# LSTM and state-space kernel: the recurrent matmuls of the second half repacked to 32 rows and 128 columns

## The reference

```python
# LSTM, T = 512 steps, h and c of [8, 512], Wh of [512, 2048]
xW = jnp.einsum('ntd,dg->ntg', x, Wx) + b
def step(carry, xw_t):
    prev_h, prev_c = carry
    a = xw_t + prev_h @ Wh
    i, f, o = sigmoid of a[:, :512], a[:, 512:1024], a[:, 1024:1536]
    g = jnp.tanh(a[:, 1536:])
    next_c = f * prev_c + i * g
    next_h = o * jnp.tanh(next_c)
x = x + lstm(x, cond, Wx, Wh, b)
# state-space layer on the new x
proj = conv(x) @ Wp + bp          # conv over time, taps from cond
B_t, C_t = softplus(proj[..., :64]), tanh(proj[..., 64:])
state = decay * state + dt * B_t * (x @ Ws + bs)
x = x + (C_t * state) @ Wo + bo
```

## Time and profile before

| | |
|---|---|
| median of 3 runs | 1964.98 us (1964.32 to 1966.52) |
| profiled execution | 1966.61 us, its span 1964.8 us |
| PE busy | 1791.0 us (91%) |
| DVE busy | 1431.2 us (73%) |
| ACT busy | 1047.5 us (53%) |
| mean granted TensorE clock | 0.994 |
| recurrent steps | first transpose of recA at 49.7 us, last at 1943.3 us |

### The profile page before, as it was taken

One profiled execution on the slowest core, in us unless ns is written; L12 is line 12 of the kernel. 1 busy time (PEld: TensorE's weight loads), 2 busy tenths in 40 slices (PEclk: granted clock), 3 DMA queues, 4 the chain that ended last, 5 costly groups with the idle time before them and its releaser, 6 DMA issues.

```text
span 1964.8 us, 90420 instructions
## 1 busy us (share of the span) xinstructions
PE 1791.0 (91%) x36274; PEld 1276.6 (65%) x36274; DVE 1431.2 (73%) x6909; ACT 1047.5 (53%) x4057; POOL 340.3 (17%) x1544
## 2 busy tenths in 40 slices
PE   6788999999999999999999999999999999999976
PEld 3555666676666666666676666666666677666755
DVE  7686667777777776777777777777777777867775
ACT  5555455555555555555555545555555555545452
POOL 1111111111111111111111111111111111111110
PEclk9999999999999999999999999999999999999998
DMA  6111111111211211111111111111111111211100
GB/s 233 49 43 47 36 46 35 51 50 36 56 51 35 62 43 49 46 46 52 45 54 39 57 44 42 55 43 48 46 53 46 44 54 32 70 43 40 51 14 23
DMA packets 112284, 98.71 MB, mean 50 GB/s; under 512 B 20097, under 2 KB 86197, under 8 KB 110838
## 3 DMA queue, kind: packets, MB, share of 16 engines
q1 hardware_dynamic: 111576, 90.83, 15.3%
q10 hardware_dynamic: 288, 2.10, 0.3%
HBM read 50.90 MB, written 41.94 MB: 47 GB/s over the span
## 4 chain that ended last, share of the span: by engine, by line
PE 45%; DVE 33%; ACT 11%; issue 5%; POOL 5%; DMA 1%; SPq 0%; POOLq 0%; DVEq 0%; ACTq 0%
PE recA L495 26%; DVE tr L848 17%; PE recB L495 9%; DVE pre L854 8%; ACT act L737 6%; POOL h L432 5%; PE pbc L540 4%; DVE hb L876 4%; PE pw L465 4%; ACT tc L747 3%; DVE prod L859 3%; ACT recB L664 1%; PE po L560 1%; DMA wpk<-in_L_cond_Wh_dram 1%; DVE acc L931 0%
## 5 line engine op out<-in xcount | busy, mean ns | idle before, releaser
L737 ACT ACTIVATE act<-pre 128x64 f32<-128x64 f32 x1024 | 263.0, 257 | 873.4 <-DVE pre L854 856.9
L495 PE MATMUL recA<-whi,hb 128*16 128x256 f16 x8176 | 514.8, 274 | 143.1 <-DVE hb L876 137.6
L495 PE MATMUL recA<-wlo,hb 128*16 128x256 f16 x8176 | 513.1, 273 | 0.0
L495 PE MATMUL recB<-wlo,hb 128*16 128x256 f16 x8176 | 513.0, 273 | 0.0
L495 PE MATMUL recB<-whi,hb 128*16 128x256 f16 x8176 | 513.0, 273 | 0.0
L495 PEld LDWEIGHTS recA<-whi,hb 128*16 128x16 f16 x8176 | 200.2, 88 | 410.3 <-DVE hb L876 354.4
L848 DVE STREAM_TRANSPOSE tr<-recA 128x256 f32<-128x256 f32 x512 | 229.9, 449 | 206.2 <-PE recA L495 205.0
L540 PE MATMUL pbc<-yt,wpk 128*128 128x256 f32 (+5 forms) x1120 | 333.3, 402 | 0.0
L432 POOL TENSOR_TENSOR h<-osc,tc 128x16 f32<-128x16 f32 x1024 | 228.2, 223 | 499.8 <-ACT tc L747 499.8
L426 POOL TENSOR_SCALAR osc<-act 128x16 f32<-128x16 f32 x512 | 105.1, 205 | 1098.4 <-ACT act L737 1098.4
L859 DVE SCALAR_TENSOR_TENSOR prod<-act 128x32 f32<-128x32 f32 x1024 | 197.1, 193 | 127.5 <-ACT act L737 127.5
(11 more groups left out here) (156 smaller groups left out, 2027.6 us busy)
## 6 DMA issues: line engine op xcount, KB each, us to landing
xw_rows<-xs SPq DMA_DIRECT2D x128, 256.0 KB, 2.2
seed<-xw_rows SPq DMA_DIRECT2D x1024, 32.0 KB, 1.9
xn<-in_x_dram SPq DMA_DIRECT2D x32, 256.0 KB
out_dram<-ot SPq DMA_DIRECT2D x32, 256.0 KB, 3.0
seed<-in_L_cond_Wh_dram ACTq DMA_DIRECT2D x2, 1024.0 KB, 6.9
wpk<-in_L_cond_Wh_dram SPq DMA_DIRECT2D x2, 1024.0 KB, 11.8
wlo<-in_L_cond_Wx_dram SPq DMA_DIRECT2D x2, 1024.0 KB, 13.1
xs<-in_L_cond_Wx_dram SPq DMA_DIRECT2D x1, 1024.0 KB, 9.3
```

The costliest lines, as they stand in the source:

```text
L495: ins = pe.matmul(rec[half][32 * j:32 * j + 2 * NB, 0:256].rearrange("p (c f) -> p c f", c=2), h[:, k, :], w[:, k, :, :].rearrange("p (c j ...
L737: act_eng.activation(act[q][:, 0:G, :].rearrange("p g n -> p (g n)"), pre[q][:, :, :, :].rearrange("p g c b -> p (g c b)"), ACT.Tanh, scal ...
```

## The change

Only half 1 is packed differently. Its two chunks no longer stand side by side as 256 columns in 16 of the 32 rows of a quadrant; chunk 2 takes rows 0 to 15 and chunk 3 rows 16 to 31 of each quadrant, and both take the same 128 columns. The matmul of one chunk has a stationary operand of 32 columns, of which 16 are zeros: `hz` has the 16 columns of the hidden state in the middle of 48, and a slice that starts at 16 (chunk 2) or 0 (chunk 3) puts them in the first or the last 16 rows. So each input chunk `k` of half 1 has four groups instead of two, of 128 moving columns instead of 256. A step has 96 matmuls instead of 64. `seeds` and `open_` of half 1 handle 128 columns, with a mask of its own. Of half 1's block with k 0, only chunk 2's part stays ahead of half 0's k 2 and 3; chunk 3's part stands behind them.

The diff, without the setup of the masks, the memsets and some renamings:

```diff
+        hz = [sb(f"hz{i}", [128, KC, 6 * NB], f16) for i in range(2)]
+        h0z = [sb(f"h0z{i}", [128, KC, 6 * NB], bf16) for i in range(2)]
...
+        tr = [sb("tr0", [128, 2, G, 4, NB]), sb("tr1", [128, G, 2, 2, NB])]
...
+        hb, h0b = ([h[:, :, 2 * NB:4 * NB] for h in hs] for hs in (hz, h0z))
+
+        WIDTH = (256, 128)
...
+        def first_seeds(eng, p, count):
+            for j in range(4):
+                own = slice(128 * j, 128 * j + 128)
+                rows = slice(2 * NB * p, 2 * NB * p + 2 * NB)
+                if count > 1:
+                    eng.dma_start(seed[32 * j:32 * j + 2 * NB, 0, p, :, :].rearrange("r q (c f) -> r (q c) f", f=128)[:, 0:count, :],
+                                  scratch[0, 0:count, rows, own].rearrange("c r f -> r c f")).then_inc(s_seed0[p], 16)
+                else:
+                    eng.dma_start(seed[32 * j + 2 * NB:32 * j + 4 * NB, 0, p, 1, 0:128],
+                                  scratch[0, KC - 1, rows, own]).then_inc(s_seed0[p], 16)
...
+                row, col = ((0, 128 * (c % 2)), (2 * NB * (c % 2), 0))[c // 2]
                 for j in range(4):
-                    sync.dma_start(seed[32 * j:32 * j + 2 * NB, z, :, c // 2, 128 * (c % 2):128 * (c % 2) + 128],
+                    sync.dma_start(seed[32 * j + row:32 * j + row + 2 * NB, z, :, c // 2, col:col + 128],
...
-            def recur(t, half, k):
+            def recur(t, half, k, parts=(0, 1)):
...
-                if k == 0:
+                if k == 0 and parts[0] == 0:
                     pe.wait_ge(s_seed[half], t + 1)
...
+                for h in (h0z if t == 0 else [hz[(t - 1) % 2]]):
+                    if half:
+                        for c in parts:
+                            for w in (whi, wlo):
+                                for j in range(4):
+                                    ins = pe.matmul(rec[1][32 * j:32 * j + 32, 0:128],
+                                                    h[:, k, 2 * NB * (1 - c):2 * NB * (1 - c) + 32], w[:, k, 4 * (2 + c) + j, :],
+                                                    start=False, stop=(k == KC - 1), skip_group_check=True)
...
                     recur(t, 0, 1)
-                    recur(t, 1, 0)
+                    recur(t, 1, 0, (0,))
                     recur(t, 0, 2)
                     recur(t, 0, 3)
+                    recur(t, 1, 0, (1,))
                     recur(t, 1, 1)
...
+                act_eng.activation(rec[q][:, 0:WIDTH[q]], seed[:, t // TS % 2, t % TS // 2, q, 0:WIDTH[q]],
+                                   ACT.Copy, scale=mask[:, q, t % 2:t % 2 + 1]).then_inc(s_seed[q], 1)
...
             wx_high(1)
+
+            act_eng.wait_ge(s_wlo, 1)
+            for c in range(KC):
+                act_eng.wait_ge(s_rows[c], 16)
+            first_seeds(act_eng, 0, 1)
...
+                order = ("p c g z b -> p (c g z b)", "p g c z b -> p (g c z b)")[q]
+                dve.transpose(tr[q][:, :, :, :, :].rearrange(order), rec[q][:, 0:WIDTH[q]]).then_inc(s_tr[q], 1)
...
+                if q:
+                    dve.tensor_tensor(pre[1][:, :, :, :], tr[1][:, :, :, 0, :],
+                                      tr[1][:, :, :, 1, :], ALU.add).then_inc(s_add[1], 1)
```

More of the change, by code:

```diff
@@ L387, in _ @@
             for p in range(TS // 2):
[L388 to L391, removed]
+                first_seeds(sync, p, KC - 1)
+                if p:
+                    first_seeds(sync, p, 1)
             for c in range(KC):
@@ L483, in first_project @@
                             x_bias(tile_bank(0, c)[:, :], c)
-            def recur(t, half, k):
+            def recur(t, half, k, parts=(0, 1)):
                 if half == 0 and k % 2 == 0:
                     pe.wait_ge(s_h[k // 2], t + 1)
-                if k == 0:
+                if k == 0 and parts[0] == 0:
                     pe.wait_ge(s_seed[half], t + 1)
[L492 to L498, removed]
+                for h in (h0z if t == 0 else [hz[(t - 1) % 2]]):
[6 more added lines that the diff above has]
+                                                    start=False, stop=(k == KC - 1), skip_group_check=True)
+                    else:
+                        for w in (whi, wlo):
+                            for j in range(4):
+                                ins = pe.matmul(rec[0][32 * j:32 * j + 2 * NB, 0:256].rearrange("p (c f) -> p c f", c=2),
+                                                h[:, k, 2 * NB:4 * NB],
+                                                w[:, k, :, :].rearrange("p (c j) f -> p c j f", j=4)[:, 0:2, j, :],
+                                                start=False, stop=(k == KC - 1), skip_group_check=True)
                 if k == KC - 1:
@@ L662, in seeds @@
                 if t < TS and t % 2 == 0 and q == 0:
[L663 to L665 removed]
+                    act_eng.wait_ge(s_seed0[t // 2], 16 * 8)
+                act_eng.activation(rec[q][:, 0:WIDTH[q]], seed[:, t // TS % 2, t % TS // 2, q, 0:WIDTH[q]],
+                                   ACT.Copy, scale=mask[:, q, t % 2:t % 2 + 1]).then_inc(s_seed[q], 1)
             def soft(key, name, src, bias, cols):
@@ L847, in open_ @@
                 dve.wait_ge(s_rec[q], t + 1)
-                dve.transpose(tr[q][:, :, :, :, :].rearrange("p c g z b -> p (c g z b)"),
-                              rec[q][:, 0:256]).then_inc(s_tr[q], 1)
+                order = ("p c g z b -> p (c g z b)", "p g c z b -> p (g c z b)")[q]
+                dve.transpose(tr[q][:, :, :, :, :].rearrange(order), rec[q][:, 0:WIDTH[q]]).then_inc(s_tr[q], 1)
             def add(t, q):
                 dve.wait_ge(s_tr[q], t + 1)
-                dve.tensor_tensor(pre[q][:, :, :, :].rearrange("p g c b -> p c g b"), tr[q][:, :, :, 0, :],
-                                  tr[q][:, :, :, 1, :], ALU.add).then_inc(s_add[q], 1)
+                if q:
+                    dve.tensor_tensor(pre[1][:, :, :, :], tr[1][:, :, :, 0, :],
+                                      tr[1][:, :, :, 1, :], ALU.add).then_inc(s_add[1], 1)
+                else:
+                    dve.tensor_tensor(pre[0][:, :, :, :].rearrange("p g c b -> p c g b"), tr[0][:, :, :, 0, :],
+                                      tr[0][:, :, :, 1, :], ALU.add).then_inc(s_add[0], 1)
             def product(t, q):
@@ L1015, in _ @@
             for z in range(2):
-                dve.tensor_reduce(mask[:, z:z + 1], diag[:, z:16:4], mybir.AxisListType.X, ALU.max).then_inc(s_mask, 1)
+                for q in range(2):
+                    dve.tensor_reduce(mask[:, q, z:z + 1], diag[:, z:16:4 - 2 * q], mybir.AxisListType.X,
+                                      ALU.max).then_inc(s_mask, 1)
             def largest(k):
@@ L1069, in _ @@
             dve.wait_ge(s_scale, 1)
-            for z in range(2):
-                dve.tensor_scalar(mask[:, z:z + 1], mask[:, z:z + 1], scale[:, 2:3], None, ALU.mult).then_inc(s_mask, 1)
+            for q in range(2):
+                dve.tensor_scalar(mask[:, q, :], mask[:, q, :], scale[:, 2:3], None, ALU.mult).then_inc(s_mask, 1)
             wh_high(2)
```

15 lines of the change are left out of this document (6 added, 9 removed).

## The result

The changed kernel takes 1935.39 us (median of 4 runs, 1934.36 to 1938.33), the one before 1964.65 (4 runs, 1964.32 to 1966.52): ratio 0.9852 [0.9835, 0.9869]. It is faster by 29 us; 37 were forecast (1928 us), and the time lies inside the forecast's own range of 1914 to 1948. The execution profiled took 1938.33 us, its span 1936.3.

The account below looks back on a forecast made before the run. In 341 steps PE waits, and the chain between recA transposes sets the time; elsewhere PE is full. 341 x 0.09 = 31 us plus 6 us gives 37: 1966.6 to 1929.6 profiled, 1928 as median; range 1914 to 1948, chance 0.77.

Parts of the forecast that it names:

- term 1: PE's filler before recA's third chunk: narrow groups 0.056 us apart, so it ends at +2.88 instead of +2.99.
- rival A: PE's narrow groups take 0.09 us each, not half the time; +0.40 a step, 2169 us; chance 0.13.
- term 2: Half 1's state: shorter ACT seeds let `tc` start at +2.12 and free the low part at +2.88, 0.09 earlier.
- terms 3 and 4: recB's transpose starts 0.13 us later, at +0.78, but takes 0.32 instead of 0.449, so product 0 stays at +1.03.
- The joint: Where product 0 on DVE follows recB's later transpose: slack of only 0.01 us, further delay there reaching both halves.
- D: Rival: group interval 0.058, transpose 0.34; 0.04 to 0.05 us lost a step, 17 us, 1948; within the range given 0.77.
- B: Rival: half 1's state comes no earlier; gain 0.02 us a step where PE waits, 1961 us; chance 0.07.
- C: Rival: full steps gain too and the joint costs nothing; 511 x 0.10 = 51 us, 1914; within the range given 0.77.
- The full steps: About 170 steps where PE's work decides: between a loss of 0.02 and a gain of 0.09 us, counted as 6 us.
- The rest: Small items: SP's 28 start transfers cause no wait; ACT's issues cost 0.3 us once, step 0's shorter groups returning about that.

Follow-up runs that it names:

- wide_seeds: The changed kernel with ACT's seeds of half 1 again 256 columns wide; 1960.49 us, ratio 0.9973 to the kernel before.
- wide_transpose: The changed kernel with DVE's transpose of half 1 again 256 columns wide; 1988.24 us, ratio 1.0114 to the kernel before.
- no_filler: The changed kernel with all of half 1's first block behind half 0; 1977.91 us, ratio 1.0062 to the kernel before.
- split_only: The kernel before, nothing packed, one of the two wide groups of half 1's first block moved behind half 0; 2010.95 us, ratio 1.0229.
- after_again: The changed kernel run again, unaltered, in a later sitting; 1934.53 us, ratio 0.984 to the kernel before.
- replan: The changed kernel with PE's beside work planned anew, same instructions in other steps; 1932.24 us, ratio 0.9832 to the kernel before.
- replan2: The changed kernel with replan's plan, but higher planner costs for `u` and `out`; 1929.65 us, ratio 0.9812 to the kernel before.

## Why the prediction came out as it did

- **The interval of narrow groups (term 1): right.** 0.056 us, over 14 groups in each of 511 steps (in step 0 part of them ran at a granted clock of 0.50). With it rival A is refuted. These groups follow neither of the two rules of the Trainium skill that spoke for it ("TensorE: Matmul & The Clock Gate", sections "Back-to-back issue gap" and "Wait — 56ns, not 53.3ns?"): four matmuls with four loads fit into 0.056 here, where the one rule gives 0.081 for a single pair and the other 0.100 for four matmuls. The four matmuls of a group, which write different quadrants, start within 0.010 us of each other in this trace, less than half of the second rule's floor for a single start.
- **The state of the second half (term 2): right in its mechanism, 0.02 too early at the end.** Seeds 354 ns (0.35), `tc` at +2.12. But `tc` lasts 216 ns where it lasted 199, and the low part starts at +2.67 instead of +2.65. These 17 ns are most of the difference between the 0.10 forecast and the 0.09 measured at +2.90. wide_seeds shows the term alone: 0.07 of 0.08.
- **The later end of recB and its shorter transpose (terms 3 and 4): right.** +0.78, 317 ns (0.32), product 0 at +1.03, second add at +1.14. The joint held, D did not come; wide_transpose, no_filler and split_only show what it costs when it gives way: 0.12, 0.10 and 0.09 a step.
- **B and C: neither.** The gain in steps with room is 0.08 to 0.085, against 0.02 (B) and 0.10 (C). The price of D was added up wrongly: 1928 + 17 is 1945, not 1948. The 3 us make the forecast's range wider than its terms; the measured time lies inside either way.
- **The full steps: this term was mis-sized.** "The middle gives 170 x 0.035 = 6 us"; the full steps measured 0. Two errors lie in it. First the bounds: a step that is full by a whole beside matmul can't gain, since its PE work grew by the 0.024 that the prediction itself worked out, and it lost 0.02; taking the middle between that and 0.09 had no row behind it. Second the count: the 341 of the earlier trace rows are the waits of more than 0.15 us, and the view does not give the length of each. PE had shorter ones in 69 more steps; what a step can gain is the smaller of 0.09 and its room. Sorted by room, 390 steps paid 31 us, and 121 paid nothing. That this equals the prediction's 341 x 0.09 = 31 us is luck: more steps gained, each somewhat less.
- **The rest:** 2.2 us at the end are put down to the clock, by the comparison above. SP's 28 transfers cost nothing that can be seen: they were issued by 56.9 us and the block for step 8 by 67.7 (forecast 65.0), and no step waits for them. Step 0 did not give back what the start cost, as the prediction had it; it took 0.4 us more, which is inside the 31.1.

So 37 became 28.5 in the profiled spans (29.3 between the medians of the runs): 6 us of full steps, 2.2 at the end, 0.4 at the start.

## What to carry to other kernels

Where two engines' work meets at one point, shorten both or neither. Here the packing alone gave nothing and the move alone cost 45 us; with both but the seeds left wide 5 us of gain remained, and with the transpose left wide the kernel was 22 us slower than before. All together gave 29 us. When a chain of steps gets shorter, list for every step how much room the busiest engine has, and count the gain step by step up to that room; beside work that was laid out for the old length of a step has to be laid out anew. When a move makes one piece later and a saving elsewhere makes it good, look for the instruction where the two meet, since from there on each ns costs about a ns in every step that has room. And before you count waits in a view, ask how short a wait it still lists.

## What the runs showed of the hardware

- The loads of 32 columns are busy for 97 ns each against 88 to 90 for 16 columns, and a group of four is issued every 56 ns: this work runs side by side and its busy time is no interval. By form, kernel after:

```profile
L515 PEld LDWEIGHTS recB<-whi,hz 128*32 128x32 f16 x16352 | 438.2, 97 | 10.1 <-issue 0.7
```

- Once, PE issued nothing for 0.86 us without a wait, inside the recurrent work, and the step took 4.48 us. Kernel after, timeline:

```profile
767.84 0.27 PE L521 MATMUL recA<-wlo,hz 128*16 128x256 f16 x1
...
768.70 0.28 PE L521 MATMUL recA<-wlo,hz 128*16 128x256 f16 x3 [0.58 <-issue]
```

Such waits inside the recurrent work, of 0.2 to 0.7 us, are listed once in this trace, three times in replan's, twice in replan2's and once in wide_seeds'. There are none in the other five traces of kernels with 96 matmuls a step (after_again's among them), and none in the three with 64. The queue of instructions moves more than before (414 packets, 6.78 MB, against 286 and 4.69), for 96 matmuls a step instead of 64. Whether the stall is a late supply of instructions was not tested and stays open. The listed waits come to 1.5 us at most in one trace.
